# A two-block transformer on one core: the first block's attention keeps its scores by query, and DMAs turn the exponentials

## The reference

```python
xn = adaln(x, c, g1, w_ada1, b_ada1)
qkv = bitlinear(xn, w_qkv, b_qkv).reshape(B, T, 3, H, hd)       # H = 16 heads, hd = 32
q, k, v = (qkv[:, :, i].transpose(0, 2, 1, 3) for i in range(3))
attn = jax.nn.softmax(jnp.einsum('bhqd,bhkd->bhqk', q, k) * hd ** (-0.5), axis=-1)
o = jnp.einsum('bhqk,bhkd->bhqd', attn, v).transpose(0, 2, 1, 3).reshape(B, T, D)
x = x + bitlinear(o, w_proj, b_proj)
```

## Time and profile before

| | us |
|---|---|
| three runs | 2233.67, 2241.35, 2239.07; median 2239.07 |
| span of the profiled execution, first to last instruction | 2237.3 |
| one iteration (first by-query score of sequence 2 to that of sequence 3) | 253 |
| its attention stage, first score to last weighing of values (602.3 to 697.0) | 94.7 |
| DMA share of the 16 engines in that stage | 19% |

### The profile page before, as it was taken

The page is one execution under the profiler, slowest core; times in us unless marked ns, Lnnn a source line. Parts: engine busy times, 40 slices in busy tenths (PEclk is TensorE's granted clock), DMA queues, the critical chain, the costliest instruction groups (busy, mean ns, idle before and its releaser), DMA issues.

```text
span 2237.3 us, 40636 instructions
## 1 busy us (share of the span) xinstructions
PE 1987.5 (89%) x13326; PEld 1003.8 (45%) x13503; DVE 1530.2 (68%) x2667; ACT 1144.3 (51%) x2090; POOL 772.1 (35%) x705
## 2 busy tenths in 40 slices
PE   4787878899989998899989998899989998899889
PEld 3354334544444444544444444544444444544434
DVE  5676657875688657875688757875788757875422
ACT  4575644754465543844466443844456443744230
POOL 2173433641255113640255113740255103741021
PEclk8899999999999999999999999999999999999989
DMA  8443533021311123031411123021321123021212
GB/s 303 144 172 109 201 127 99 26 104 62 129 49 58 67 96 99 26 104 62 128 49 58 67 96 99 26 104 53 118 68 53 72 96 99 26 71 44 94 38 94
DMA packets 85529, 200.87 MB, mean 90 GB/s; under 512 B 7612, under 2 KB 48864, under 8 KB 73144
## 3 DMA queue, kind: packets, MB, share of 16 engines
q1 hardware_dynamic: 77528, 174.88, 23.4%
q10 hardware_dynamic: 7776, 23.10, 2.8%
HBM read 161.97 MB, written 35.72 MB: 88 GB/s over the span
## 4 chain that ended last, share of the span: by engine, by line
PE 42%; issue 28%; POOL 17%; DVE 7%; ACT 5%; DMA 0%; POOLq 0%; ACTq 0%; SPq 0%; DVEq 0%
POOL memory L1257 12%; PE banks L1435 8%; PE banks L1434 8%; PE banks L1436 8%; PE banks L1327 5%; PE banks L1392 5%; DVE memory L1012 2%; PE banks L1309 1%; POOL memory L1004 1%; PE banks L1378 1%; POOL memory L1180 1%; ACT memory L1045 1%; POOL memory L1474 1%; DVE memory L1019 1%; DVE memory L1027 1%
## 5 line engine op out<-in xcount | busy, mean ns | idle before, releaser
L1435 PE MATMUL banks<-memory 128*128 128x512 bf16 x1512 | 574.2, 380 | 19.5 <-DVE memory L1506 6.6
L1434 PE MATMUL banks<-memory 128*128 128x512 bf16 x1438 | 550.4, 383 | 23.1 <-DVE memory L1559 7.8
L1436 PE MATMUL banks<-memory 128*128 128x512 bf16 x1491 | 566.4, 380 | 1.3
L1257 POOL TENSOR_TENSOR memory<-memory 128x512 bf16<-128x512 f32 x332 | 375.7, 1152 | 366.5 <-ACT memory L1246 365.2
L1246 ACT ACTIVATE memory<-banks 128x512 f32<-128x512 f32 x512 | 290.9, 599 | 129.6 <-PE banks L1239 127.2
L1660 POOL TENSOR_TENSOR memory<-memory 128x512 bf16<-128x512 f32 x128 | 144.7, 1132 | 487.6 <-DVE memory L1655 487.6
L1189 PE MATMUL banks<-memory 96*128 96x512 bf16 x512 | 186.7, 392 | 73.6 <-DVE memory L1201 39.1
L1434 PEld LDWEIGHTS banks<-memory 128*128 128x128 bf16 x1536 | 149.0, 97 | 217.1 <-issue 15.5
L1201 DVE TENSOR_REDUCE memory<-banks 128x1 f32<-128x512 f32 x320 | 207.8, 680 | 37.6 <-PE banks L1189 37.4
L1436 PEld LDWEIGHTS banks<-memory 128*128 128x128 bf16 x1536 | 148.5, 97 | 186.7 <-issue 4.3
L1435 PEld LDWEIGHTS banks<-memory 128*128 128x128 bf16 x1536 | 152.1, 99 | 165.4 <-issue 3.8
(11 more groups left out here) (176 smaller groups left out, 2951.2 us busy)
## 6 DMA issues: line engine op xcount, KB each, us to landing
memory<-weight_parts SPq DMA_DIRECT2D x80, 1024.0 KB, 4.9
memory<-head_parts SPq DMA_DIRECT2D x192, 128.0 KB, 2.8
head_parts<-memory SPq DMA_DIRECT2D x64, 256.0 KB, 2.8
memory<-in_x SPq DMA_DIRECT2D x32, 256.0 KB, 3.3
memory<-ada_rows SPq DMA_DIRECT2D x16, 512.0 KB, 4.5
memory<-in_L_cond_w_fc ACTq DMA_DIRECT2D x2, 4096.0 KB, 14.3
memory<-in_L_cond_mlp_w SPq DMA_DIRECT2D x8, 1024.0 KB, 7.7
weight_parts<-memory SPq DMA_DIRECT2D x8, 1024.0 KB, 4.9
```

The source lines that it names most:

```text
L1257: eng.tensor_tensor(prob_lo[:, e % RING], expo[:, e % RING], prob_hi[:, e % RING], ALU.subtract).then_inc(ok.sem, 1)
L1434: pe.matmul(bank, lh, rh, start=(k == 0), stop=False)
L1435: pe.matmul(bank, lh, rl, start=False, stop=False)
L1436: mm = pe.matmul(bank, ll, rh, start=False, stop=(k == KC - 1))
```

## The change

Steps 3 and 4 are taken out. The scores stay as they come from `scores_by_query`, queries on the partitions. The head scale is folded into the queries (`copy_scales` has a second output `scale_q`, and the query bias is scaled once). A pair p is two tiles of the same head; there are 32.

- `maxima` (DVE) takes every pair in one instruction and signals `pair_max`, which ACT waits for.
- `exponential` (ACT) reads the two tiles with the maximum as its bias per partition and writes a 128 x 1024 fp32 row into one of three buffers `expo` (laid over `x0` and `ada`).
- `prob_high_dve` (DVE) copies the upper halves of all 32 pairs into `split[:, :, 0]` and `prob_low` (POOL) subtracts the rests of all 32 pairs into `split[:, :, 1]`, both 128 x 1024.
- `turn_pair` (SP) issues one transposing DMA a pair: 128 x 2048 bf16, 512 KB, from one of four `split` buffers into one of four `turned` buffers (two of them laid over `x_next`), 16 blocks of 128 x 128.
- `weigh_values` (PE) takes half a head at a time, with the same 16 matmuls a pair, from `turned`.
- Since `x_next` and `x0` are overlaid, `save_rows` writes the residual to memory (1 MB) before the first transpose and `bring_rows` loads it again after the last; the load of `ada` moves behind that.

In the diff, cut to its core, the tables of slots are left out but for the new ones.

```diff
+EXPS, SPLITS, TURNED = 3, 4, 4
-STACKS = 3
+STACKS = 2
...
+EXP_AT = {2 * p + 2: p for p in range(PAIRS)}
+SPLIT_AT = {2 * p + 4: p for p in range(PAIRS)}
+TURN_PAIR_AT = {2 * p + 6: p for p in range(PAIRS)}
+VALUES_AT = {2 * p + 1 + HOLD: p for p in range(PAIRS)}
+HIGH_DVE = tuple(range(PAIRS))
+LOW_DVE = ()
+LOW_POOL = [p for p in range(PAIRS) if p not in LOW_DVE]
...
+        def maxima(dve, i, p):
+            b = ready(dve, plan0, last_tile(p), i)
+            dve.tensor_reduce(neg_max[:, p % 16], banks[:, b - 1:b + 1], AX.X, ALU.max,
+                              negate=True).then_inc(pair_max.sem, 1)
...
+        def exponential(act, i, p):
+            b, _ = plan0[last_tile(p)]
+            act.wait_ge(pair_max.sem, pair_max(i, p + 1))
+            if p >= EXPS:
+                split_of(act, i, p - EXPS, True)
+                split_of(act, i, p - EXPS, False)
+            for t in range(2):
+                ins = act.activation(expo[p % EXPS][:, t * T:(t + 1) * T], banks[:, b - 1 + t], ACT.Exp,
+                                     bias=neg_max[:, p % 16, t:t + 1])
+            ins.then_inc(free[b].sem, 1)
...
+        def split_free(eng, i, p):
+            done(eng, plan0, last_tile(p), i)
+            if p >= SPLITS:
+                s = pair_turned[p % SPLITS]
+                eng.wait_ge(s.sem, s(i, 16 * (p // SPLITS)))
...
+        def prob_high_dve(dve, i, p):
+            split_free(dve, i, p)
+            dve.tensor_copy(split[:, p % SPLITS, 0], expo_hi[p % EXPS]).then_inc(high_dve.sem, 1)
+
+        def prob_low(eng, i, p, ok):
+            split_free(eng, i, p)
+            eng.tensor_tensor(split[:, p % SPLITS, 1], expo[p % EXPS], expo_hi[p % EXPS],
+                              ALU.subtract).then_inc(ok.sem, 1)
+
+        def turn_pair(sp, i, p):
+            split_of(sp, i, p, True)
+            sp.sem_inc(paced, 1)
+            split_of(sp, i, p, False)
+            sp.sem_inc(paced, 1)
+            if p >= TURNED:
+                if p % 2 == 0:
+                    sp.wait_ge(half_read.sem, half_read(i, (p - TURNED) // 2 + 1))
+                else:
+                    ready(sp, plan0, ("o", (p - TURNED) // 2), i)
             else:
...
+                sp.wait_ge(rows_saved.sem, rows_saved(i, 16))
+            sp.sem_inc(paced, 1)
+            sp.dma_start_transpose(turned_rows[p % TURNED], split[:, p % SPLITS].rearrange("p s n -> p (s n)")
+                                   ).then_inc(pair_turned[p % TURNED].sem, 16)
...
+        def save_rows(sp, i):
+            sp.wait_ge(x0_bias.sem, x0_bias(i, TT))
+            sp.dma_start(rows_d, x_next).then_inc(rows_saved.sem, 16)
...
+            s = pair_turned[p % TURNED]
+            pe.wait_ge(s.sem, s(i, 16 * (p // TURNED + 1)))
...
+            act.activation(scale_bc, banks[:, b], ACT.Copy)
+            act.activation(scale_q, banks[:, b], ACT.Copy, scale=HEAD_SCALE).then_inc(free[b].sem, 1)
```

More of the change, by code:

```diff
@@ L1204, in turn_maxima @@
-        def turn_maxima(pe, i, c):
-            done(pe, plan0, ("s", c, HEADS - 1), i)
-            b = take(pe, plan0, ("max", c), i)
-            for t in range(TT):
-                mm = pe.transpose(banks[0:G, b, t * P:(t + 1) * P], neg_max[:, c % 2, t], ident)
-            mm.then_inc(full[b].sem, 1)
-        def max_high(act, i, c):
-            b = ready(act, plan0, ("max", c), i)
-            if c > 0:
-                act.wait_ge(max_in[c - 1].sem, max_in[c - 1](i, 32))
-            act.activation(max_hi[0:G], banks[0:G, b], ACT.Copy).then_inc(max_parts.sem, 1)
@@ L1232, in scores_by_key @@
-        def scores_by_key(pe, i, c, n):
-            j, kt = divmod(n, TT)
-            if n == 0:
-                pe.wait_ge(max_in[c].sem, max_in[c](i, 32))
-            b = take(pe, plan0, ("st", c, n), i)
-            rows = STACK + MAX_ROWS
-            pe.matmul(banks[:, b], k_stack[0:rows, c % STACKS, j, kt * P:(kt + 1) * P],
-                      q_stack[0:rows, c % STACKS, j], start=True, stop=True).then_inc(full[b].sem, 1)
-        def exponential(act, i, e):
-            b = ready(act, plan0, ("st", *divmod(e, HEADS)), i)
-            if e >= RING and e % TT == 0:
-                ready(act, plan0, ("o", (e - RING) // TT), i)
-            act.activation(expo[:, e % RING], banks[:, b], ACT.Exp, scale=HEAD_SCALE).then_inc(free[b].sem, 1)
@@ L1248, in first @@
-        def first(i):
-            return isinstance(i, int) and i == 0
-        def rests(i):
-            return (FIRST_POOL, FIRST_LOW_DVE) if first(i) else (LOW_POOL, LOW_DVE)
-        def prob_low(eng, i, e, ok):
-            done(eng, plan0, ("st", *divmod(e, HEADS)), i)
-            eng.tensor_tensor(prob_lo[:, e % RING], expo[:, e % RING], prob_hi[:, e % RING],
-                              ALU.subtract).then_inc(ok.sem, 1)
-        def weigh_values(pe, i, h):
-            if h == 0:
-                pe.wait_ge(v_lo.sem, v_lo(i, TT))
-            last = TT * h + TT - 1
-            for ok, tiles in zip((lo_pool, lo_dve), rests(i)):
-                n = count_to(tiles, last)
-                if n or not first(i):
-                    pe.wait_ge(ok.sem, n if first(i) else ok(i, n))
-            b = take(pe, plan0, ("o", h), i)
-            for t in range(TT):
-                at = t * 2 * LOW
-                for kt in range(TT):
-                    for part in (prob_hi, prob_lo):
-                        mm = pe.matmul(banks[:, b, at:at + VALUE], part[:, (h * TT + kt) % RING, t * P:(t + 1) * P],
-                                       values[:, kt, h], start=(kt == 0 and part is prob_hi),
-                                       stop=(kt == TT - 1 and part is prob_lo))
-            mm.then_inc(full[b].sem, 1)
@@ new lines, in save_rows, with bring_rows, weigh_values @@
+        def save_rows(sp, i):
+            sp.wait_ge(x0_bias.sem, x0_bias(i, TT))
+            sp.dma_start(rows_d, x_next).then_inc(rows_saved.sem, 16)
+        def bring_rows(sp, i):
+            for high in (True, False):
+                split_of(sp, i, PAIRS - 2, high)
+                sp.sem_inc(paced, 1)
+            sp.dma_start(x0, rows_d).then_inc(rows_back.sem, 16)
+        def weigh_values(pe, i, p):
+            h, half = divmod(p, 2)
+            if p == 0:
+                pe.wait_ge(v_lo.sem, v_lo(i, TT))
+            s = pair_turned[p % TURNED]
+            pe.wait_ge(s.sem, s(i, 16 * (p // TURNED + 1)))
+            b = take(pe, plan0, ("o", h), i) if half == 0 else plan0["o", h][0]
+            for t in range(2):
+                at = (2 * half + t) * 2 * LOW
+                for kt in range(TT):
+                    for part in range(2):
+                        mm = pe.matmul(banks[:, b, at:at + VALUE], turned[p % TURNED][:, part, t, kt],
+                                       values[:, kt, h], start=(kt == 0 and part == 0),
+                                       stop=(kt == TT - 1 and part == 1))
+            mm.then_inc(full[b].sem if half else half_read.sem, 1)
@@ L1812, in both @@
                         value_low(pool, i, t)
[L1813 to L1819 removed]
+                for p in range(PAIRS):
+                    if j is not None and p == RSTD_AT:
+                        rstd_of1(pool, j, 1)
+                    if i is not None and p in LOW_POOL:
+                        prob_low(pool, i, p, low_pool)
                 for n, job in enumerate(M):
```

326 lines of the change are left out of this document (138 added, 188 removed).

## The result

The changed kernel takes 2343.82 us (median of four runs, 2339.32 to 2345.16), the kernel before, beside it, 2237.77 (four runs, 2233.67 to 2241.35). The ratio is 1.0466 with a 95% interval of 1.0447 to 1.0485: 106 us, or 4.7%, slower. The forecast was 2351.

A forecast was written before the change was run, and what follows sets the result against it. The prediction took VectorE's list to pace the attention stages, TensorE the rest: 2237.3 + 105 (seven stages) + 6.5 (iteration 0) = 2348.8, with 1.8 for the median of the runs 2351 us; 8-in-10 range 2245 to 2540.

The forecast's parts named there:

- the pair's time: Attention stage: each pair takes 2.97 us, with VectorE's copy and GpSimd's rest excluding one another.
- 0.78 us a pair of other work: VectorE in the attention stage: work other than maximum and copy, 25 us a stage or 0.78 a pair.
- its 2.69: Pair's time in us without exclusion of copy and rest: 1.22 maximum + 0.69 copy + 0.78 other work.
- +15.0 a stage: Each of seven attention stages grows from 94.7 to 109.7 us, together +105.
- the 5.9 us of VectorE's waits that were kept: Attention stage: VectorE's waits for the second block's steps and late queries, 15.0 us idle now, 5.9 kept in the sum.
- The tail: Stage's end after the last maximum: exponentials 1.3, rest 1.96, copy 0.69, landing 4.5, values 0.6, together 9.05 us.
- Iteration 0's +6.5: First stage: pair's time covered by waits for weights, only the tail grows, from 2.5 us, so +6.5.
- The limit: Transposing DMA: anything below about 2.9 us each gives the same time, as a pair takes 2.97; price taken 2.3.
- the prediction's bound of 9.1 us: Transposing DMA: 9.1 us each if it went in 256-byte pieces, each taking as long as 1 KB; kernel about 3920.
- The rival: Transposes set the stage's pace, if slower than 2.9 us each: 2510 us at 3.6 each; chance 0.25.
- The mild case: Copies fit into gaps and hardly meet rests: pair 2.69, stage 101, kernel 2289 us; chance 0.12.
- A faster kernel: Copy and its wait together under 0.49 us, stage below 94.7: kernel 2233 or 2192 us; chance 0.10.

The follow-up runs named there:

- with few rests: Changed kernel with GpSimd subtracting only 4 of a sequence's 32 rests, transposes kept: 2300.40 us, ratio 1.0275 to the kernel before.
- with few rests and plain DMAs: Changed kernel with only 4 of 32 rests, and plain DMAs of the same bytes for the transposing ones: 2224.37 us, ratio 0.993 to the kernel before.
- Plain DMAs: Changed kernel with plain DMAs of the same 512 KB for the transposing ones, probabilities not turned: 2335.39 us, ratio 1.042 to the kernel before.
- taking 12 us off VectorE: Changed kernel with every other upper-half copy moved to ScalarE: 2322.33 us, ratio 1.0371 to the kernel before; with plain DMAs as well, 2294.08 us.
- The added one: Changed kernel with one more VectorE reduction a pair, a maximum over the upper halves before the copy: 2569.85 us, ratio 1.1469 to the kernel before.

## Why the prediction was right, by its steps

**The mechanism held, the pair's time in part by luck.** Copy and rest exclude one another, VectorE's list stretched by that sets the stage, and the transposes hide behind it. The prediction set copy, other work and maximum behind the rest and got 2.97 us a pair; 2.99 was measured, but as the mean of 3.54 where other work fills VectorE and 2.73 where copies meet rests. Neither part takes the formula's time. The Trainium skill (SBUF — State Buffer, Who interferes with whom) says that a copy that uses both of VectorE's ports and GpSimd hold the shared ports by turns; the trace agrees, with 0.68 us where no rest runs and up to 2.25 where one does.

**The prices.** Copy 0.69 us unblocked: 0.68. Maximum 1.22: 1.21. Rest 1.96: 1.89 undisturbed. VectorE's own work 86 us: with few rests its records add up to 88.1 (39.0 for maxima, 22.6 for copies, 26.5 for the rest), but they overlap by 9% and it is busy for 80.0. The prediction scaled VectorE's busy time up to the sum of its records to get 0.78 us a pair of other work, and then put copy, other work and maximum end to end with no overlap, which makes its pair some 0.2 us too long. Against that the exclusion also stretches the late queries' and the second block's two-source steps, which the prediction did not reckon: in the changed stage four steps of L1112 take 1.59 us each and four of L1499 1.09, where 0.79 and 0.77 were their means before. Nor did it reckon VectorE's idle time among the pairs: 4.1 us in the changed stage, 7.0 with few rests and plain DMAs, where its 2.69 was measured as 2.65. These errors nearly cancel in the pair's time.

**The sum was too high in a stage and too low in iteration 0.** Its +15.0 a stage was measured as 12.1 an iteration. The term that was mis-sized is the 5.9 us of VectorE's waits that were kept beside the pairs: only 2.5 of them are there, as the first maximum ends at 4.1 us and not at 1.6; VectorE's 4.1 us of waits among the pairs are inside the 92.8. The tail measured 8.45 where 9.05 was reckoned, and `save_rows` nothing where 1 us was. Iteration 0's +6.5 was measured as 21.7, the largest miss of a term: "the pair's time is covered there by the waits for weights" failed. Plain DMAs take 12.3 us off its stage of 155.6, leaving out half of the rests 8.7, and plain DMAs with 4 of 32 rests bring it to 134.5, where it was 129.9 before. The misses, 7 x 15.0 = 105 against 82.6 and 6.5 against 21.7, have opposite signs and left the total only 7 us too high; that closeness is luck too.

**The transposes were hidden by little.** The limit was put at 2.9 us and the price at 2.3. With few rests they are issued 2.51 us apart from the ninth on, 0.2 below the 2.73 that a pair takes where the changed stage's list is full. They go in pieces of 256 bytes, as the prediction's bound of 9.1 us had it, but each piece costs far less than was assumed there. The rival was wrong for this kernel. Where VectorE was relieved, plain DMAs shortened the stage by 2.5 to 8.0 us, but the pairs' pace only with few rests, and the other gains lay behind the last maximum. Landing takes 3.9 us, not 4.5. The estimate from the Trainium skill (DMA: Bandwidth & Descriptors, Latency and other measured facts), 2.0 us, was below the pace that the trace shows; that 16 blocks might go one after another by the figure in the Trainium skill (VectorE: DVE Perf Modes, The three transpose paths) was not borne out, since all 16 land within 3.9.

**The signs it named.** Copies' mean 0.7 to 1.5 us, long beside rests: 1.06, yes. Stage 105 to 115, VectorE over 80%: 105.3 and 89%, yes. TensorE near 60%: 70%, since its clock was lower and its records longer. A wait of 7 us before the last weighing: no, three of the last four weighings share 4.0 us. No wait for `pair_turned` in the middle: 0.8 us on GpSimd in sequence 2's stage, and TensorE's matmuls wait 2.4 us for landings ahead of those last four, so nearly.

**The other rivals.** The mild case needed copies that hardly meet rests; 19 of 32 in sequence 2's stage take more than 0.70 us. A faster kernel needed copy and wait under 0.49 us; the copy alone takes 0.68. Both fell. Without 28 of the 32 rests and without the turning the stage is 92.6 and the kernel 0.7% faster: that is all the change returns with most of its new work left out.

## What to carry to other kernels

When work is split between VectorE and GpSimd on the same data, look in the trace for durations of one shape with a long maximum over a tight median: if two instructions exclude one another, their times add up on both engines, and changing the order of the two moves the wait and doesn't remove it. Look for what lies just under the limit before counting a relief: here taking 12 us off VectorE returned 3, and 5.5 with plain DMAs as well. And split a stage's mean before trusting a formula for it: 2.99 us a pair agreed with 2.97, and neither of its two parts did. Sum the first iteration by itself, with the resources that only it shares.

## What the runs showed of the hardware that was not expected

A transposing DMA costs more than its bytes. 512 KB from SBUF to SBUF hold SP's queue for 1.70 us and land in 3.9, and a stage of them brings the DMA share to 1.00; plain DMAs of the same bytes hold the queue for 0.465 us, land in 3.0 and leave the share at 0.59.

A reduction is not stretched by GpSimd, even when it reads SBUF. The added one, all 256 times (shortest, median, longest ns):

```profile
L1222 DVE TENSOR_REDUCE memory<-memory x256: 1200/1205/1219, 75.7 to 2287.8; 128x1 f32<-128x1024 bf16 x128
```

It runs beside the same rests that stretch the copies from 0.68 to 2.25 us. This too stands in the Trainium skill (SBUF — State Buffer, Who interferes with whom), which names copies among what can take the shared ports and reductions among what never does on this chip; the trace agrees.

An exponential with its bias per partition takes 684 ns where the one without took 595, 6 us a stage on ScalarE, hidden here. The Trainium skill (ScalarE: Activation LUTs, What ACT_TABLE_LOAD costs) puts each such operand at about 93 ns; the trace's 89 agree.

TensorE's granted clock is 0.85 in the changed stage, 0.98 before. From 731.7 to 734.2 TensorE stood still for a landing; at 734.84 a matmul of 512 columns takes 0.62 us, where it took 0.38 at 731.34, and at 740.92 it takes 0.38 again. The stretch between (columns as above) was granted half of the clock, 1.2 of 2.4 GHz:

```profile
735.00:737.80 2.80, 2.80 (x22) 1.44 (x20) 0.26 (x2) 0.55 (x2) 1.42 (x1) 0.50 0.96 216
```

Little of the stage can come from it, as VectorE's maxima wait only 3.3 us for scores.
